# Mixture of experts in DRAM: eight planes written plainly instead of one sum, and added at the start of attention 1

## The reference

```python
scores = softmax(xt @ Wr)                      # xt: 4096 tokens x 128
G, idx = top_k(scores.T, 1024)                 # per expert
h = gelu(einsum('ekd,edh->ekh', xt[idx], W1) + b1[:, None, :])
X_e = einsum('ekh,ehd->ekd', h, W2) + b2[:, None, :]
contrib = (G[..., None] * X_e).reshape(E * k, D)
out = zeros((4096, 128)).at[idx.reshape(-1)].add(contrib)
x = x + gb * out
h = layernorm(x) * (1 + ca) + sa               # second layer starts
```

## Time and profile before

| | us |
|---|---|
| median of three runs | 1327.55 |
| the profiled execution | 1333.13 |
| its span | 1331.0 |
| PE busy | 1001.3 (75%) |
| DVE busy | 809.2 (61%) |
| ACT busy | 611.0 (46%) |
| POOL busy | 424.9 (32%) |
| first gather of the experts starts | 742.09 |
| last scatter ends | 966.99 |

### The profile page before, as it was taken

One profiled execution on the slowest core, in us unless ns is written; L12 is line 12 of the kernel. 1 busy time (PEld: TensorE's weight loads), 2 busy tenths in 40 slices (PEclk: granted clock), 3 DMA queues, 4 the chain that ended last, 5 costly groups with the idle time before them and its releaser, 6 DMA issues. The chain is left out here.

```text
span 1331.0 us, 24972 instructions
## 1 busy us (share of the span) xinstructions
PE 1001.3 (75%) x8508; PEld 684.6 (51%) x8508; DVE 809.2 (61%) x1812; ACT 611.0 (46%) x2042; POOL 424.9 (32%) x312
## 2 busy tenths in 40 slices
PE   5679899898989898986612487776428989877765
PEld 2446556565656565655602355453316666655554
DVE  5755867666666757563656515112235889749995
ACT  2465776767575757563201132311115555543422
POOL 2432333323232423221000568787710121200221
PEclk8699999999999999997555789888759999978867
DMA  6563343434343434340401124346320000000000
GB/s 194 139 178 97 87 111 99 110 95 112 80 113 87 111 98 112 97 102 17 123 0 60 29 52 74 61 58 149 28 67 1 1 1 1 1 0 9 16 16 24
DMA packets 89872, 93.61 MB, mean 70 GB/s; under 512 B 18768, under 2 KB 63296, under 8 KB 89808
## 3 DMA queue, kind: packets, MB, share of 16 engines
q1 hardware_dynamic: 78544, 84.12, 24.1%
q0 software_dynamic: 11264, 8.66, 4.8%
HBM read 24.36 MB, written 10.70 MB: 26 GB/s over the span
## 5 line engine op out<-in xcount | busy, mean ns | idle before, releaser
L797 POOL TENSOR_TENSOR qk_cos<-qk_raw,const 128x512 f32<-128x512 f32 x128 | 181.0, 1415 | 356.2 <-ACT qk_raw L562 356.2
L548 ACT ACTIVATE prob<-psS,neg_max 128x96 f32<-128x96 f32 x512 | 167.5, 342 | 75.0 <-DVE neg_max L643 74.8
L415 PE MATMUL psQ<-a_xnT,weights 128*128 128x512 f32 x246 | 141.8, 659 | 17.3 <-ACT v_tok L567 16.6
L523 PEld LDWEIGHTS psO<-probT,v_windows 96*64 96x64 f32 x2048 | 72.8, 142 | 122.9 <-ACT probT L620 97.8
L1463 POOL DMA_INDIRECT sums<-ex_y,ex_index x64 | 102.4, 1601 | 36.3 <-issue 18.6
L523 PE MATMUL psO<-probT,v_windows 96*64 96x64 f32 x2048 | 90.9, 233 | 25.7 <-ACT probT L620 25.3
L658 DVE TENSOR_TENSOR qk_roped<-qk_cos,qk_swapped 128x512 f32<-128x512 f32 x128 | 105.9, 827 | 5.1 <-DVE qk_swapped L649 4.6
L1453 POOL DMA_INDIRECT ex_rows<-rows,ex_index x64 | 67.0, 1046 | 129.4 <-DMA ex_index<-lists 110.2
L548 ACT ACTIVATION_READ_ACCUMULATOR prob<-psS,neg_max 128x1 f32 x512 | 106.0, 207 | 0.0
L1398 ACT ACTIVATE ex_hidden<-ex_psH,ex_b 128x512 f32<-128x512 f32 x64 | 43.5, 687 | 125.2 <-DVE ex_index L1527 53.3
L620 ACT COPY probT<-psT 96x512 f32<-96x512 f32 x128 | 74.8, 584 | 55.4 <-PE psT L503 55.3
(11 more groups left out here) (317 smaller groups left out, 1964.0 us busy)
## 6 DMA issues: line engine op xcount, KB each, us to landing
qk_swapped<-qk_raw SPq DMA_DIRECT2D x512, 64.0 KB, 2.0
v_windows<-v_tok SPq DMA_DIRECT2D x32, 384.0 KB, 4.4
v_windows<-v_tok SPq DMA_DIRECT2D x32, 256.0 KB, 3.6
mod<-mod_rows SPq DMA_DIRECT2D x12, 512.0 KB, 6.2
ex_w<-in_L_ffn_W SPq DMA_DIRECT2D x16, 256.0 KB
v_windows<-v_tok SPq DMA_DIRECT2D x32, 96.0 KB, 2.1
rows<-rt_h SPq DMA_DIRECT2D x8, 256.0 KB, 2.4
sums<-rt_zeros SPq DMA_DIRECT2D x8, 256.0 KB, 2.7
```

Source lines behind the costliest of these rows:

```text
L415: last = nc.tensor.matmul(bank, k.wqkvT[:, col:col + P], xnT[:, :], start=True, stop=True)
L523: ins = nc.tensor.matmul(psO[D * j:D * j + D, u % 2, i * P + a * HALF:i * P + (a + 1) * HALF], vw[:, par, a, t, hd], probT[:, 2 * j + i, a ...
L548: last = nc.scalar.activation(prob[:, s, 2 * j + i, :], psS[:, s, j, i * KW:(i + 1) * KW], ACT.Exp, bias=nmax[:, s, 2 * j + i:2 * j + i + ...
L797: nc.gpsimd.tensor_tensor(rcos[:, half, :], raw[:, half, :], k.const[:, K_COS:K_COS + T], ALU.mult).then_inc(cos_done, 1)
```

## The change

The DRAM tensor `sums` becomes `planes`, eight planes of 4096 x 128, one for each expert. Each expert stores its rows in its own plane, without adding; the wait for the other expert's scatter goes. The row in the plane is computed from the token's number with four bit operations more on DVE (`own_at`), and the plane's layout has the four tiles of a partition next to each other, 2 KB in a piece. All planes have to be zero before, 64 stores of 256 KB, half of them before the store of the scores and half behind it. In attention 1, sequence 0 of all planes is loaded and added by DVE in seven steps. Of the other sequences plane 0 is loaded, and POOL issues transfers that add planes 1 to 7 to it in SBUF: first for sequences 1 to 3, after `root_one(0)`, then for 4 to 7, after `root_one(2)`. A round is one plane; it waits until the round before has landed.

```diff
@@ router, SP @@
             def body(b, s2):
                 sp.wait_ge(h_ready, b + 1)
                 sp.dma_start(rows[b][:, :, 0:C], h[:, s2, :, :]).then_inc(h_stored[s2], 16)
-                sp.wait_ge(zeroed, 1)
-                sp.dma_start(sums[b], zeros[:, :, :]).then_inc(cleared, 16)
...
             pairs(sp, body)
+            sp.wait_ge(zeroed, 1)
+            for n in range(E0 * B // 2):
+                sp.dma_start(planes[n], zeros[:, :, :]).then_inc(cleared, 16)
             sp.wait_ge(scores_ready, 1)
             sp.dma_start(k.rows.rearrange("(n p) c -> p n c", p=P)[:, :, C:ROW], s[:, :, :]).then_inc(scores_stored, 16)
             for s2 in range(2):
                 sp.wait_ge(h_stored[s2], 16 * B // 2)
-            sp.wait_ge(cleared, 16 * B)
+            for n in range(E0 * B // 2, E0 * B):
+                sp.dma_start(planes[n], zeros[:, :, :]).then_inc(cleared, 16)
+            sp.wait_ge(cleared, 16 * E0 * B)
             sp.wait_ge(scores_stored, 16)
@@ experts, POOL @@
             def scatter(e, par, turn):
 
-                wait(pool, scattered[1 - par], 16 * SLOTS * (turn + par))
                 for n in range(SLOTS):
...
-                    nc.gpsimd.indirect_dma_start(k.sums, bass.IndirectOffsetOnAxis(ap=index2[:, par, n:n + 1], axis=0),
-                                                 y[:, par, n, :], None, compute_op=ALU.add).then_inc(scattered[par], 16)
+                    nc.gpsimd.indirect_dma_start(k.planes, bass.IndirectOffsetOnAxis(ap=index2[:, par, n:n + 1], axis=0),
+                                                 y[:, par, n, :], None, compute_op=ALU.bypass).then_inc(scattered[par], 16)
@@ experts, DVE @@
+            def own_at(token, at, tile, lane, e):
+
+                place.mark(nc.vector.tensor_scalar(tile, token, 7, TILES - 1, ALU.logical_shift_right, ALU.bitwise_and))
+                place.mark(nc.vector.tensor_scalar(lane, token, P - 1, 2, ALU.bitwise_and, ALU.logical_shift_left))
+                dve.wait_ge(place.sem, place.mark(nc.vector.tensor_scalar(at, token, (B - 1) * T, None, ALU.bitwise_and)))
+                dve.wait_ge(place.sem, place.mark(nc.vector.tensor_tensor(lane, lane, tile, ALU.bitwise_or)))
+                nc.vector.scalar_tensor_tensor(out=at, in0=at, scalar=plane[:, bass.ds(e, 1)], in1=lane,
+                                               op0=ALU.bitwise_or, op1=ALU.bitwise_or).then_inc(kept, 1)
...
-                nc.vector.tensor_copy(index2[:, par, :], index[:, par, :]).then_inc(kept, 1)
+                own_at(index[:, par, :], index2[:, par, :], tile_at[:, par, :], lane_at[:, par, :], e)
@@ attention 1, SP @@
-            for i, (lo, hi) in enumerate(((0, 2), (2, B))):
-                sp.dma_start(k.total[:, lo:hi, :, :].rearrange("p b t c -> p (b t) c"),
-                             k.sums[lo * T:hi * T].rearrange("(t p) c -> p t c", p=P)).then_inc(sums_ld[i], 16)
+            planes = k.planes.rearrange("(e b p t) c -> e p b t c", e=E0, t=TILES, p=P)
+            sp.dma_start(k.total[:, 0, :, :], planes[0][:, 0, :, :]).then_inc(first_ld, 16)
+            for e in range(1, E0):
+                sp.dma_start(first_sums[:, e - 1, :, :], planes[e][:, 0, :, :]).then_inc(first_ld, 16)
+            sp.dma_start(k.total[:, 1:B, :, :], planes[0][:, 1:B, :, :]).then_inc(plane_ld, 16)
@@ attention 1, POOL; LATER = ((1, 2, 3), (4, 5, 6, 7)) @@
+            def add_planes(i):
+                for e in range(1, E0):
+                    wait(pool, plane_added, 16 * added(i, e - 1))
+                    for b in LATER[i]:
+                        nc.gpsimd.dma_start(k.total[:, b, :, :], planes[e][:, b, :, :], accum_op=ALU.add).then_inc(plane_added, 16)
+
             norm.root_one(pool, 0)
+            pool.wait_ge(plane_ld, 16)
+            add_planes(0)
             norm.root_one(pool, 1)
 
             def body(b, par, first, next1, next2):
                 if next2:
                     norm.root_one(pool, b + 2)
+                if b == 0:
+                    add_planes(1)
@@ attention 1, DVE @@
             def add_experts(b):
 
+                if b > 0:
+                    dve.wait_ge(plane_added, 16 * added(b // 4, E0 - 1))
...
-            dve.wait_ge(sums_ld[0], 16)
+            dve.wait_ge(first_ld, 16 * E0)
+            for e in range(1, E0):
+                dve.wait_ge(own.sem, own.mark(nc.vector.tensor_tensor(k.total[:, 0, :, :], k.total[:, 0, :, :], first_sums[:, e - 1, :, :], ALU.add)))
             add_experts(0)
```

More of the change, by code:

```diff
@@ L1010, in _ @@
             rows = k.rows.rearrange("(b t p) c -> b p t c", t=TILES, p=P)
-            sums = k.sums.rearrange("(b t p) c -> b p t c", t=TILES, p=P)
+            planes = k.planes.rearrange("(n p t) c -> n p t c", t=TILES, p=P)
             def body(b, s2):
@@ L1286, in phase_experts @@
         b1 = sb("ex_b1", [P, 2, KD])
+        plane, tile_at, lane_at = sb("ex_plane", [P, E0], U32), sb("ex_tile_at", [P, 2, SLOTS], U32), sb("ex_lane_at", [P, 2, SLOTS], U32)
         w1, w2 = sb("ex_w1", [C, 2, DI]), sb("ex_w2", [P, 2, KD, C])
@@ L1308, in phase_experts @@
         own = Tally(sem("own"))
+        place = Tally(sem("place"), 4)
         block = ctx.enter_context(nc.Block())
@@ L1484, in _ @@
             own.turn(0)
+            own.mark(nc.vector.tensor_scalar(plane[:, :], k.const[:, K_IOTA:K_IOTA + E0], float(B * T), None, ALU.mult))
             own.mark(nc.vector.tensor_copy(iota[:, :], k.const[:, K_IOTA:K_IOTA + SPLIT]))
@@ L1519, in _ @@
                 last.then_inc(ids_ready, 1)
+            def own_at(token, at, tile, lane, e):
[5 more added lines that the diff above has]
+                                               op0=ALU.bitwise_or, op1=ALU.bitwise_or).then_inc(kept, 1)
             def keep(e, par, turn):
+                place.turn(e)
                 dve.wait_ge(gathered[par], 16 * SLOTS * (turn + 1))
@@ L1565, in phase_attention1 @@
         mul = sb("a1_mul", [P, TILES, C])
-        sums_ld = [sem(f"sums_ld{i}") for i in range(2)]
+        first_ld, plane_ld, plane_added = sem("first_ld"), sem("plane_ld"), sem("plane_added")
+        LATER = ((1, 2, 3), (4, 5, 6, 7))
+        added = lambda i, e: len(LATER[i]) * e + (len(LATER[0]) * (E0 - 1) if i else 0)
+        first_sums = sb("a1_first", [P, E0 - 1, TILES, C])
         h, hT = sb("a1_h", [P, TILES, C]), sb("a1_hT", [C, T])
@@ L1829, in body @@
                     if u == 2 and next2:
-                        if isinstance(b, int) and b == 0:
-                            dve.wait_ge(sums_ld[1], 16)
                         add_experts(b + 2)
@@ L2090, in build @@
                 dram = lambda name, shape, dt: nc.dram_tensor(name, shape, dt, kind="Internal").ap()
-                k.rows, k.sums, k.lists = dram("rows", (B * T, ROW), F32), dram("sums", (B * T, C), F32), dram("lists", (E0, CAP), U32)
+                k.rows, k.planes, k.lists = dram("rows", (B * T, ROW), F32), dram("planes", (E0 * B * T, C), F32), dram("lists", (E0, CAP), U32)
                 phase_router(nc, k)
```

## The result

The changed kernel takes **1420.68 us** (median of four runs, 1413.91 to 1422.09), the kernel before beside it 1329.04 (1325.54 to 1335.77): a ratio of **1.069** [1.065, 1.073]. The forecast was 1395, the range 1365 to 1450. The profiled executions have spans of 1331.0 and 1418.5, so 87.5 us are to be explained, where the prediction had 67.5.

What follows compares the result with a forecast made beforehand. POOL's issuing was taken to bound the experts stage. Terms -39 + 61.3 + 43.2 + 2 + 0 = +67.5 on the profiled 1333.1 gave 1400.6; with the median 5.6 lower, the forecast was 1395 us, range 1365 to 1450.

Steps and rivals of the forecast that it cites:

- Main mechanism: Attention 1: POOL's two blocks of adding rounds make DVE wait, +61.3 and +43.2 us.
- Router, 0: Router: 64 zero stores stay covered by the threshold search on DVE and PE, 0 us, bounds 0 and +6.
- Scatter at the gather's price: Experts: without addition, eight scatters issue in the gathers' 10.1 us instead of 14.9.
- The rival of dear plain scatters: Experts: plain scatters cost what adding ones do, giving 1432 us; chance 0.18.
- Experts, -39: Experts stage: cheaper plain scatters save 29 us in batches 0 to 5 and shorten the tail from 39 to 29.
- the main case: Whole kernel: the forecast of 1395 us with its own range 1374 to 1422; chance 0.61.
- First wait, +61.3: Attention 1, before DVE's second step: 14.0 us of loads and start, plus seven rounds of three, 54.3, less 7.0.
- n x I + S + L: Attention 1: time of a round of n adding transfers; issue I 1.55, data S 1.3, landing L 1.8 us.
- Second wait, +43.2: Attention 1, after rstd 2: seven rounds of four, 65.1 us, delay rstd 3, which had come 21.9 after rstd 2.
- Second start of PE, +2: Attention 1: PE restarts at its 1.2 GHz clock level after idling, 0 to 5 us, taken as +2.
- Additions at half the load's rate: Attention 1: an adding transfer reads two sources, so S is 1.5 us, twice the plain 0.73; sum 3 us higher.
- the rival of 85: Attention 1: additions run at the scatter's 85 GB/s, S 3.1 us, rounds 12.7 and 15.8, giving 1475; chance 0.10.

Runs made afterwards that it cites:

- D: Fourth chip: kernel before 1329.32 us, changed kernel 1421.50, without additions 1316.62, gathers of 32 bytes a row 1416.19, gathers waiting for PE's second product 1436.50.
- B: Second chip: kernel before 1317.33 us; changed kernel without additions 1284.44, with 32-byte gathers 1386.77, with adding scatters 1429.21, with gathers waiting for PE's second product 1414.82.
- A: Chip of the first runs: kernel before 1329.04 us, changed kernel 1420.68.
- C: Third chip: kernel before, median 1328.12 us, changed kernel 1424.92, and a version adding planes 0 to 5 on DVE during the experts, 1350.09.
- the gathers held: Changed kernel, but POOL starts the gathers for expert e+2 only after PE's second product of expert e: 1414.82 us on B, 1436.50 on D.
- the early sum: Changed kernel with gathers waiting for PE's second product; DVE adds planes 0 to 5 during the experts, attention 1 only 6 and 7: 1350.09 us, ratio 1.020, on C.
- the short gathers: Changed kernel with each gather from expert 2 on fetching 32 bytes a row instead of 544: 1386.77 us on B, 1416.19 on D.

## Why the prediction was right, and where it was not

**Main mechanism: right.** The loss is the two blocks of adding transfers. Without the additions the rest takes 359.9 us on D instead of 460.2, and the kernel is 12.7 us faster than before (1316.6 against 1329.3); with them it is 92 slower (one run each). So they cost some 100 us, the loads and DVE's additions for sequence 0 included, and the predicted first and second wait make 61.3 + 43.2 = 104.5.

**Router, 0: right.** SP's stores are issued by 698.6, and the phase ends at its old time.

**Scatter at the gather's price: right.** 0.98 against 1.55 to 1.60, and the experiment that puts the addition alone back gives 1.62. The rival of dear plain scatters falls.

**Experts, -39: the step that failed** is "POOL at 20 us an expert stays above PE's 16.5". It holds on B, where the batches are 20.8 us apart. It does not hold on A, C and D: there PE's second product stretches beside POOL's plain transfers, an expert takes PE 25 us, and POOL waits 46.2 us for y. The term came out at -15.4. The 16.5 was read from the earlier trace rows, in a window in which the second products of experts 2 to 6 lie beside adding scatters; in the changed kernel they lie beside gathers. A busy time measured beside one neighbour was taken for the time beside another. And the record of before held a warning that my window, from 785 on, all but cut off, the one second product that begins beside gathers, expert 0's:

```profile
772.23 2.62 PE L1367 MATMUL ex_psY<-ex_w,ex_hidden 128*128 128x128 f32 x22
777.37 0.27 PE L1367 MATMUL ex_psY<-ex_w,ex_hidden 128*128 128x128 f32 x1 [2.53 <-issue]
...
780.88 7.23 PE L1367 MATMUL ex_psY<-ex_w,ex_hidden 128*128 128x128 f32 x39 [1.07 <-issue]
```

It takes 15.9 us, with 5.1 of "issue". The term is off by +23.6, more than the 20 by which the whole difference of the spans was missed (87.6 against 67.5); the second wait gave 6.6 back. The other 5.6 us of the miss come from forecasting from the median, 5.6 below the profiled run, while the changed kernel's profiled run lies at its median. So the time lies inside the range, and by 1.3 us inside that of the main case, with a large term wrong: that much is luck.

**First wait, +61.3: measured +65.3.** A round of three takes 7.9 us (976.41 to 1023.79 is six of them), predicted 7.75, but by luck: the form of the sum, n x I + S + L, was wrong. The issue is 0.88 us for one transfer (2.64 for three), not 1.55, and it hides behind the data. What repeats is the data, 1.9 us for each transfer (5.7 for three), where S was one time 1.3. That an accumulating transfer must cost POOL what an indexed one does was the wrong row to lean on. The remaining 4 us are the start. The rounds began 18.3 us after SP's first load, not 14.0, though the loads' data had ended by 972, 13.9 after it: root_one(0) stands ahead of the rounds in POOL's queue and itself waits for DVE's seven additions (5.05 us). I had called these hidden; they are not, they hold up the rounds that should hide them.

**Second wait, +43.2: measured +36.6.** A round of four takes 9.2, predicted 9.3. But rstd 3 stands behind the last round's issue in the queue, not behind its landing, so it is six rounds and one issue (1065.92 to 1123.44, 57.5, the record of rstd 3 overlapping that of the issue), not seven rounds. Its own 2.37 us take 1.4 of the gain away.

**Second start of PE, +2:** the remainder is 0.3 shorter than before, so 0.

**Additions at half the load's rate or the scatter's 85 GB/s.** They run at 158 GB/s for a DMA share of 0.98, 0.44 of the load's rate, so the rival of 85 falls. S by this rate is 1.7 us, not 1.3, near the 1.5 that the prediction gave for a second source read. A packet of 2 KB takes 178 ns in the adding transfers and 84 in the plain loads before them (medians of the trace), a factor of 2.1. This fits a second read; no run parts it from the arithmetic. A fourth transfer adds 9.2 - 7.9 = 1.3 us to a round here; over all nine records with additions a round of three takes 7.5 to 8.3 us and one of four 9.2 to 9.4. Issue to landing is 5.8 us (median of 49, the DMA part of the page), most of it behind the others of the round, at least 3.8, where a zero store of the same 256 KB takes 3.3. The Trainium skill (DMA: Bandwidth & Descriptors, Anatomy of one DMA — SWDGE (gpsimd) path) fits a plain transfer of POOL's at 2.0 us plus its bytes at 436 GB/s, by which 256 KB would be an estimated 2.6 us. No run here has a plain direct transfer on POOL.

**What stays open** is why PE is held back on A, C and D and not on B. Shown on the first three: it is not the program and not the bytes, it comes beside plain gathers and beside plain scatters, and in 40 of 41 cases it ends when a batch of these is through. A pause of PE before the product does not keep it away: with the gathers held, on D and in the early sum, products stretch right behind waits of 4.6 to 9.3 us for rows. What was never seen stretched is a product beside adding scatters, ten of them in the two records of the kernel before (experts 2 to 6), each 7.3 us. Their issues lie 1.9 us apart, those of plain transfers 1.25. (One product beside plain scatters stayed at 7.3 as well, expert 7's in the early sum, while a single scatter took 4.59 us.) So the pace of POOL's transfers is a rival cause, and it is untested: the adding scatter was put back only on B, where nothing stretches. Expert 1's product there (796.3 to 803.6 on A) is not against it, with adding scatters for 3.4 us and gathers only for the last 3.6. It is also the second product that is hit, with a matmul every 0.12 us, and hardly the first, with one every 0.48. A supply of PE's instructions that POOL's transfers slow would fit, but the page's queues for instructions show no transfer to match, and no run here measured the supply. It is argued, not shown. Nor did the changed kernel itself run on B; that it would be near 1387 there rests on the short gathers, which differ from it by 5 us on D.

## What to carry to other kernels

A round of three accumulating DMAs of 256 KB costs 8 us when it waits for the one before, and 5.7 of these are data at less than half the load's rate; without the wait at most 2.2 us a round could be saved. Seven rounds on the path are 55 us, and they belong where another engine has slack (here, DVE while the experts run), not at the head of a phase. When a change moves an engine's work beside other work, its busy time beside the old neighbour is not its time beside the new one; look for the one place where it already ran beside the new one, and read that. And compare kernels on one chip: the same program took 184 and 219 us in one stage on two chips, and a run on the wrong one would have "proved" that the gathers' bytes slow the matmuls.

## What was not expected of the hardware

- On three of five chips a run of 64 matmuls of 128x128x128 stretches from 7.3 to as much as 18.8 us, a few of them issued one by one at multiples of about 0.7 us, until POOL's batch of plain indirect transfers is through, with the granted clock still at 1.00 when it begins and at 0.50 behind most of the long ones. On a fourth chip it did not occur in four records; on the fifth no product lay beside a batch in a way that could tell. It is worth 32 us of this kernel without the additions (1284.4 against 1316.6), where the kernel before differs by 12 between the same chips (1317.3 against 1329.3).
- The addition in an indirect scatter costs POOL 0.63 us each in issue (1618 against 989 ns), and turns its 16 packets of 4 KB into 128 of 512 bytes. In a direct transfer of 256 KB three issues lie in 2.64 us, 0.88 each, less than a plain scatter's 0.98 or a gather's 0.94; their records overlap, and a single one has a median of 1.22.
- Adding direct transfers from DRAM into SBUF move 158 GB/s where plain loads move 358. In a chain of rounds each costs 1.6 us of start, 1.9 a transfer of 256 KB in threes, and 0.6 until the next.
